# Sums of squares of the scan's norm: VectorE adds the blocks of both directions, and the output products stand between the one-column products

## The reference

```python
y = ys.transpose(1, 0, 2, 3) + D[None, None, :, None] * xh     # the scan's output and the skip term
y = y.reshape(b, l, D_INNER)
yz = y * jax.nn.silu(z)
yz = yz * jax.lax.rsqrt(jnp.mean(yz * yz, -1, keepdims=True) + 1e-05) * norm_w
return yz @ out_w
```

## Time and profile before

| | |
|---|---|
| median of 3 runs | 764.42 us (764.05 to 764.9) |
| the profiled execution's own time | 764.11 us |
| its span in the trace | 762.3 us |
| mean granted PE clock | 0.912 of full speed |
| PE busy | 642.0 us, 84% |
| DVE busy | 485.5 us, 64% |
| ACT busy | 371.9 us, 49% |
| POOL busy | 279.3 us, 37% |

### The profile page before, as it was taken

How to read it: one execution, slowest core, us unless ns; L and a number is a source line. 1 busy time by engine, 2 the same in 40 slices (tenths; PEclk the granted TensorE clock), 3 DMA queues, 4 the chain that set the end, 5 groups by cost and what they waited for, 6 DMA issues and landing times.

```text
span 762.3 us, 13399 instructions
## 1 busy us (share of the span) xinstructions
PE 642.0 (84%) x4916; PEld 575.3 (75%) x4916; DVE 485.5 (64%) x1254; ACT 371.9 (49%) x857; POOL 279.3 (37%) x293
## 2 busy tenths in 40 slices
PE   2329899898989936739899999799989999999994
PEld 2328776578989722328788888698989999999993
DVE  3368779562250788674877774388358777777752
ACT  0027876771342538456566543341136565565551
POOL 2534515344020335013432434101313675675633
PEclk9759999996999956659999999789979999999998
DMA  7810000215000091300000002103155677688843
GB/s 220 192 45 5 2 1 1 94 39 148 1 1 1 4 253 29 114 0 5 3 5 4 3 6 84 45 1 115 37 223 172 179 241 244 188 240 229 190 130 67
DMA packets 30412, 67.89 MB, mean 89 GB/s; under 512 B 6890, under 2 KB 20755, under 8 KB 28011
## 3 DMA queue, kind: packets, MB, share of 16 engines
q0 software_dynamic: 13200, 48.20, 21.8%
q1 hardware_dynamic: 17147, 18.84, 9.1%
HBM read 60.90 MB, written 6.61 MB: 89 GB/s over the span
## 4 chain that ended last, share of the span: by engine, by line
PE 46%; DVE 6%; ACT 2%; issue 2%; POOL 1%; another core or an unknown queue 1%; POOLq 0%; DVEq 0%; ACTq 0%
PE bank L1856 10%; PE bank L1816 4%; PE bank L1820 4%; PE bank L1819 4%; PE bank L1818 4%; PE bank L1817 4%; PE bank L1736 2%; PE bank L1672 2%; PE bank L1715 2%; DVE amx L2423 1%; PE bank L1692 1%; PE bank L1722 1%; PE bank L1634 1%; PE bank L1698 1%; DVE big L2429 1%
## 5 line engine op out<-in xcount | busy, mean ns | idle before, releaser
L2498 DVE TENSOR_SCALAR big<-bank 128x256 f32<-128x256 f32 (+1 forms) x126 | 52.1, 414 | 60.5 <-PE bank L1820 55.1
L1271 ACT ACTIVATE big<-bank 128x256 f32<-128x256 f32 (+1 forms) x126 | 47.6, 379 | 57.5 <-PE bank L1820 53.8
L797 POOL TENSOR_TENSOR big<-big,arc 128x423 f32<-128x423 f32 (+1 forms) x48 | 37.8, 814 | 77.5 <-DVE arc L2443 77.5
L824 POOL DMA_INDIRECT total<-big,goal x32 | 53.6, 1675 | 24.0 <-issue 17.3
L1816 PE MATMUL bank<-x_lead,w_lead 128*128 128x256 f32 x192 | 56.4, 294 | 0.0
L1819 PE MATMUL bank<-x_both,w_lead 128*128 128x256 f32 x192 | 54.5, 284 | 0.0
L1820 PE MATMUL bank<-x_both,w_rest 128*128 128x256 f32 x192 | 54.1, 282 | 0.0
L1818 PE MATMUL bank<-x_lead,w_rest 128*128 128x256 f32 x192 | 54.0, 281 | 0.0
L1817 PE MATMUL bank<-x_rest,w_lead 128*128 128x256 f32 x192 | 53.8, 280 | 0.0
L831 POOL DMA_INDIRECT big<-x_rows,origin x32 | 33.4, 1042 | 48.9 <-DVE goal L2555 23.2
L2509 DVE SCALAR_TENSOR_TENSOR big<-big 128x256 f32<-128x256 f32 (+1 forms) x126 | 50.3, 410 | 0.0
(11 more groups left out here) (532 smaller groups left out, 2010.2 us busy)
## 6 DMA issues: line engine op xcount, KB each, us to landing
big<-in_patches SPq DMA_DIRECT2D x1, 1536.0 KB, 7.6
areg<-in_e_gate_up SPq DMA_DIRECT2D x1, 1536.0 KB, 6.6
shared_lead<-in_e_gate_up POOLq DMA_DIRECT2D x1, 1536.0 KB, 7.0
wreg<-in_ffn_w SPq DMA_DIRECT2D x1, 1152.0 KB
ffw_lead<-in_ffn_w POOLq DMA_DIRECT2D x1, 1152.0 KB, 7.1
out<-total SPq DMA_DIRECT2D x2, 423.0 KB
wreg<-in_in_w SPq DMA_DIRECT2D x2, 419.0 KB
wreg<-in_in_w SPq DMA_DIRECT2D x4, 209.5 KB
```

The lines of the kernel that those rows point to most:

```text
L824: pool.indirect_dma_start(out=total, in_=YS[:, j % 2, q * D:(q + 1) * D], in_offset=None, out_offset=bass.IndirectOffsetOnAxis(ap=goal[:, ...
L1271: nc.scalar.activation(GS[:, n % 3, 0:w], bank[2 * (n % 2)][:, 0:w], ACT.Silu).then_inc(S["g_silu"], 1)
L2498: v.tensor_scalar(UM[:, n % 3, 0:w], bank[2 * (n % 2) + 1][:, 0:w], 10.0, -10.0, ALU.min, ALU.max).then_inc(S["u_clip"], 1)
```

## The change

Three things are changed. DVE now adds the three blocks of SQ for both directions, in three parts (`SQ_PARTS`): direction 0 whole, with its first addition after `skip(12)` and its second after `skip(13)`, inside the scan loop; then behind the loop direction 1's first 846 tokens and its last 282. PE makes 9 one-column products per direction, 18 in place of 36. And PE's order is other: direction 0's one-column products, then `out_project0(4)` to `out_project0(8)`, then direction 1's one-column products. ACT's instructions are the same, as are POOL's and SP's.

```diff
+        SQ_PARTS = ((0, slice(0, T)), (1, slice(0, 6 * L)), (1, slice(6 * L, T)))
...
             pe.wait_ge(S["gm_ready"], len(ITS))
-            pe.wait_ge(S["sq_added"], 1)
+
+            def sums_of_squares(d, t):
+
+                pe.wait_ge(S["sq_added"], 1 + d * (1 if (t + 1) * P <= 6 * L else 2))
+                return mm(bank[7][0:rows(t), 2 * t + d:2 * t + d + 1], SQ[:, d * KD, t * P:t * P + rows(t)], ones[:, 0:1], start=True, stop=True)
+
             for t in range(TT):
-                mm(bank[7][0:rows(t), 2 * t:2 * t + 1], SQ[:, 0, t * P:t * P + rows(t)], ones[:, 0:1], start=True, stop=True)
-            pe.wait_ge(S["sq_ready"], 3 * KD)
-            for t in range(TT):
-                for k in range(KD):
-                    last = mm(bank[7][0:rows(t), 2 * t + 1:2 * t + 2], SQ[:, KD + k, t * P:t * P + rows(t)], ones[:, 0:1],
-                              start=k == 0, stop=k == KD - 1)
-            last.then_inc(S["ss_ready"], 1)
+                sums_of_squares(0, t)
             pe.wait_ge(S["dtx_ready"], XUSE(len(ITS)))
             for t in range(4, TT):
                 out_project0(t)
+            for t in range(TT):
+                last = sums_of_squares(1, t)
+            last.then_inc(S["ss_ready"], 1)
             pe.wait_ge(S["yz_ready"], len(ITS))
...
-            def add_squares(d):
-
-                o = SQ[:, d * KD, :]
-                dve.wait_ge(S["sq_ready"], d * KD + 2)
-                st.add(v.tensor_tensor(o, o, SQ[:, d * KD + 1, :], ALU.add))
-                st.wait()
-                dve.wait_ge(S["sq_ready"], d * KD + 3)
-                v.tensor_tensor(o, o, SQ[:, d * KD + 2, :], ALU.add).then_inc(S["sq_added"], 1)
+            def add_squares(part, k):
+
+                d, cols = SQ_PARTS[part]
+                o = SQ[:, d * KD, cols]
+                dve.wait_ge(S["sq_ready"], part * KD + k + 1)
+                if k == 1:
+                    st.add(v.tensor_tensor(o, o, SQ[:, d * KD + k, cols], ALU.add))
+                else:
+                    st.wait()
+                    v.tensor_tensor(o, o, SQ[:, d * KD + k, cols], ALU.add).then_inc(S["sq_added"], 1)
...
                 skip(n)
-            add_squares(0)
+                if n in (12, 13):
+                    add_squares(0, n - 11)
+            for part in (1, 2):
+                add_squares(part, 1)
+                add_squares(part, 2)
             dve.wait_ge(S["ss_std"], 2)
```

More of the change, by code:

```diff
@@ L981, in _, with squares @@
             nc.scalar.activation(ET.rearrange("p a b -> p (a b)"), bank[5][:, 0:RD // 4 * R], ACT.Exp, scale=-1.0).then_inc(S["e_ready"], 1)
-            def squares(d, cols):
+            def squares(part):
+                d, cols = SQ_PARTS[part]
                 act.wait_ge(S["yz_ready"], 8 * d + cols.stop // L)
@@ L1020, in _ @@
                 if n == 11:
-                    squares(0, slice(0, T))
-            squares(1, slice(0, 6 * L))
-            squares(1, slice(6 * L, T))
+                    squares(0)
+            squares(1)
+            squares(2)
             act.wait_ge(S["ss_ready"], 1)
```

## The result

The changed kernel takes 751.70 us (median of 4 runs, 751.13 to 754.20), where the kernel before took 764.66 beside it (764.05 to 766.46). The ratio is 0.9833, with a 95% interval of 0.9805 to 0.9861: faster, by 12.8 us (10.6 to 14.9). The medians themselves lie 13.0 apart. I had forecast 750.0, a gain of 14.4.

The account below looks back on a forecast made before the run. PE's program order alone was taken to set the time from 174 to 203.5; 174.11 + 1.98 + 4.88 + 1.98 + 0.3 starts out_project1 at 183.25, 14.40 us earlier. From 764.11 that gives 749.7, forecast as 750.0, range 748.5 to 753.4.

Parts of the forecast that it names:

- The wait at 174.4: PE's wait for direction 0's sum goes: PE continues at 174.11 and not at 176.65, 2.54 us less.
- The one-column products: PE's two groups of one-column products take 2 x 1.98 us at full clock instead of 14.60, 10.64 less.
- The output products between: PE's 30 rows between the one-column groups take 4.88 us instead of 6.40, 1.52 less; their order costs nothing.
- The waits: Each one-column product's own, already met semaphore wait on PE: 0.3 us taken in all, bounds 0 and 3.6.
- The additions in the scan: DVE's two additions in the scan loop delay back(15) by 0 to 0.6 us; 0 taken.
- Direction 1's additions: DVE's additions behind skip(15) end by 177.3, before PE wants them at 180.97.
- point 6: Direction 1's additions: without the 30 rows of output products as cover, PE would stand 1.2 us.
- The norm: ACT and DVE need 0.8 us after PE's last row; normed(0) waits 1.24 anyway, so it fits, 0.3 to spare.
- B: Clock falls over a one-column stretch, returns after some 3 us of output products: once 751.5, twice 753.0; chance 0.34.
- from there all is as before: From out_project1's start, at 183.25 instead of 197.65, nothing else changes, so the whole 14.40 us arrives.
- C: Clock stays low through the one-column products, 758.1, or their rows get no cheaper, 753.3; chance 0.10.
- rival D: The scan slips, POOL going first at both additions: 0.6 us, at most 1.4, so 750.6 to 751.4; chance 0.05.

Follow-up runs that it names:

- adds_behind_loop: The changed kernel with direction 0's two additions put back behind the scan loop; 749.72 us, 0.9881 of the kernel before.
- old_order: The changed kernel with all 18 one-column products ahead of out_project0(4) to (8); 747.98 us, 0.9873 of the kernel before.
- one_wait: The changed kernel with only three waits on sq_added and none on the other 15 one-column products; 753.50 us, 0.9858 of the kernel before.
- after_third: The changed kernel measured a third time, without edit; 753.53 us, 0.9846 of the kernel before.
- ff_early_again: The changed kernel, its first feed-forward products no longer waiting for the last transposed tiles, measured once more; 748.96 us, 0.9777 of the kernel before.
- pe_adds: The changed kernel with direction 1's three blocks summed on PE again, without DVE's four additions for it; 751.92 us, 0.9916 of the kernel before.
- early_add_only: The kernel before with only direction 0's two additions moved behind skip(12) and skip(13); 762.74 us, 0.9969 of the kernel before.

## Why the prediction was right, and where it was off

1. *The wait at 174.4,* priced at 2.54: the idle time is gone, as predicted. The way from the start of the 12 rows to the first one-column row went from 4.49 to 2.05 us, 2.44 less (the 12 rows take 2.05 and not 1.95). `adds_behind_loop` has it back.
2. *The one-column products,* priced at 1.98 us a group at full clock: 1.89 and 1.88, 0.105 a row and not 0.110. That is 10.83 less than the 14.60 before, for 10.64.
3. *The output products between,* 4.88: they took 4.96. "Their order costs nothing" was true but missed what the order is worth: in `old_order` all 18 one-column products ahead of them brought the clock down, and the stretch was 1.8 us longer.
4. *The waits,* 0.3: nothing, as `one_wait` shows.
5. *The additions in the scan:* 1.32 each with DVE first, the last `mix` 0.95 us nearer to `back(15)` and not 1.25, PE not delayed. So in the profiles. POOL's product took 2.06 and 2.02 us behind DVE's addition, for 1.03 alone, so the rule that the prediction cites from the Trainium skill, page "SBUF — State Buffer", section "Who interferes with whom" (the first to issue keeps the other out for its whole instruction), showed again.
6. *Direction 1's additions:* 1.03, 1.68, 0.45 and 0.45, the last ended at 179.48, 4.2 us ahead of PE's second group. In `old_order` even the cover was not needed: the 1.2 us of point 6 took the first product to need the last addition, and it is the seventh.
7. *The norm:* ACT's `normed(0)` began 1.32 us after `out_project1`, for 1.24 before. It fits.

The sum of the stretch, 14.40 predicted, came out at 2.44 + 10.83 + 1.44 = 14.71 in its profile, and the same in all six profiles of this order (10.78 or 10.79 us, with `one_wait` and the two with early feed-forward products). Of the rivals, none was seen in the changed kernel itself. The median of 751.70 is by its number nearer to B with one fall (751.5) than to the forecast, but that is chance: the clock was full where B has its fall. B was right as a mechanism in neighbours of the kernel: the clock falls with one-column products alone. My price for one such fall, 1.5 us, fits `old_order`; `adds_behind_loop` shows that it can be 3.0.

What was off is the step "from there all is as before". The whole kernel gained 13.0, 12.3, 12.6 and (as `one_wait`) 11.4 us in the medians, some 2 less than the stretch. The prediction allowed a us or so either way for half clock later on and priced nothing of it. In the profiles, 1.6 us on average are lost behind `out_project1`. The likeliest place is the fall at the feed-forward products, which all four profiles of the changed kernel have and one of three of the kernel before, and which is in none of the three with early feed-forward products. The range held the measured time, but its upper part was there for B and C: that a loss of another kind fitted into it was luck.

This does not settle all of it, since with the early feed-forward products in both kernels the medians still lie only 12.8 us apart. Within a kernel the slower runs tend to have the lower granted clock: in `after_third` the profiled run took 749.34 us at 0.922, and the five others 751.85 at 0.919 to 756.53 at 0.915; in `ff_early_again` it took 745.85 at 0.925, and the others 747.5 to 749.9 at 0.921 to 0.923. So the runs that were not profiled had more half clock than the profiled one, and no profile shows where. No profile shows a slip in the scan, rival D, though how long the clock is at half ahead of the stretch varies (its start lies between 170.4 and 175.7 us in the profiles of the changed order, between 171.7 and 173.1 in those of the kernel before). Why the changed kernel's runs would meet more half clock than their profiles stays open.

## What to carry to other kernels

A product whose moving operand has one column cost as much here as its weights take to load (0.105 us a row, for 0.110 of loading), and a run of them of 3 us and more lowered TensorE's clock even with no idle time; so halve them by adding on an engine that has time, and put dense products between what remains: of the 14.7 us won here, 7.5 are the rows gone (at their price at half clock), 2.4 the wait, and 4.8 the clock. A wait of 2.3 to 2.5 us on TensorE can cost another 1.6 to 3.0 in half clock behind it, as it did here with one-column products behind the wait, or with 2 us of transposes ahead of it in seven profiles of eleven; look at the granted clock behind each wait, not at its idle time alone. And check a gain that a trace shows against the medians: here some 2 of 14.7 us did not arrive.

## What was not expected of the hardware

The clock fell after 3.0, 3.1 and 3.8 us of one-column products in a row with TensorE never idle (`pe_adds`, `early_add_only`, `old_order`), though the profile calls it 100% busy there. At half clock, 14 us of them did not bring it back in the kernel before. Twice 1.9 us of them, with 5 us of output products between, left it full in six profiles of six.

Where the clock falls with an unchanged kernel varies by run, and with it the time: at the start of the feed-forward products it did so in one of three profiles of the kernel before. The times of the kernel before went from 763.6 to 769.7 us in one session, and its median from 758 to 766 between sessions on the same chip.
